# An attention and mixture-of-experts kernel: wk moved to the front of SyncE's queue, q before v in the first batch, and the differences of the rounded chunks moved from GpSimd to VectorE

## The reference, cut to what matters

```python
x = x + xattn(layernorm(x), ctx_768, Wq, Wk, Wv, Wo, bo)   # 8 batches of 256 tokens, width 256, context width 192, 4 heads
x = x + ffn(layernorm(x), ...)

def xattn(q, kv, ...):
    qp, kp, vp = q @ Wq.T, kv @ Wk.T, kv @ Wv.T            # split in 4 heads of 64
    attn = softmax(einsum('bhqd,bhkd->bhqk', qh, kh) * 64 ** -0.5)
    return merged(attn @ vh) @ Wo.T + bo

def ffn(x, ...):                                           # 2048 tokens, 32 experts, 4 chosen for a token
    scores = softmax(xf @ gw + gb)                         # 8 groups of 4 experts; the best 4 groups are kept,
    weights, indices = top4 of the kept experts            # then the best 4 experts
    y = sum over chosen experts of weight * ((silu(xf @ w1 + b1) * (xf @ w3 + b3)) @ w2 + b2)
    z = (silu(xf @ sw1 + sb1) * (xf @ sw3 + sb3)) @ sw2 + sb2     # the shared expert, for every token
    return y + z
```

## Time and profile before

| what | value |
|---|---|
| median of 3 executions | 361.5 us (359.2 to 362.98) |
| the profiled execution, its time | 360.53 us |
| the profiled execution, its span | 358.8 us |
| busy share of PE, DVE, ACT, POOL | 88%, 71%, 54%, 50% |
| mean granted TensorE clock | 0.957 of full speed |
| DMA | 68.96 MB, 192 GB/s in the mean |

### The profile page before, as it was taken

The page is one execution under the profiler, slowest core; times in us unless marked ns, Lnnn a source line. Parts: engine busy times, 40 slices in busy tenths (PEclk is TensorE's granted clock), DMA queues, the critical chain, the costliest instruction groups (busy, mean ns, idle before and its releaser), DMA issues.

```text
span 358.8 us, 9631 instructions
## 1 busy us (share of the span) xinstructions
PE 314.1 (88%) x2240; PEld 265.0 (74%) x2241; DVE 255.0 (71%) x865; ACT 194.1 (54%) x632; POOL 179.8 (50%) x221
## 2 busy tenths in 40 slices
PE   2998999999999999799999999999999999996000
PEld 1785887978788787478877888998989898985000
DVE  5489777878787785964795666776676676764775
ACT  2386777878777576327312565665656565653000
POOL 4620402656555575715562065666666576656500
PEclk9999999999999999699999999999999999999655
DMA  6899265585822236402424355656666565658798
GB/s 175 264 395 377 82 202 178 221 287 185 311 74 91 76 127 241 172 18 76 143 93 124 99 171 170 194 175 195 184 192 185 167 212 171 191 179 306 272 412 301
DMA packets 33782, 68.96 MB, mean 192 GB/s; under 512 B 5339, under 2 KB 26108, under 8 KB 32092
## 3 DMA queue, kind: packets, MB, share of 16 engines
q1 hardware_dynamic: 26364, 46.95, 40.6%
q0 software_dynamic: 6960, 21.11, 15.9%
q10 hardware_dynamic: 432, 0.59, 0.6%
HBM read 39.87 MB, written 28.77 MB: 191 GB/s over the span
## 4 chain that ended last, share of the span: by engine, by line
PE 76%; DMA 9%; DVE 5%; issue 3%; ACT 2%; SPq 2%; ACTq 1%; POOL 0%; POOLq 0%; DVEq 0%
PE psS L1235 11%; PE psF L103 7%; PE psF L1244 5%; PE psS L1224 5%; PE psF L1235 5%; DMA xn2T_all<-dispatch 4%; PE psS L103 4%; PE psS L985 4%; PE psF L1020 4%; PE psS L993 4%; PE psF L1034 3%; PE psF L939 3%; PE psF L1127 3%; PE psS L1093 3%; DMA w<-shares 2%
## 5 line engine op out<-in xcount | busy, mean ns | idle before, releaser
L677 POOL DMA_INDIRECT shares<-xn2T_all,e_number x81 | 86.2, 1064 | 60.1 <-issue 25.5
L626 POOL DMA_INDIRECT dispatch<-work,slot_now x64 | 64.7, 1010 | 59.2 <-issue 22.2
L1235 PE MATMUL psS<-work,arena 128*128 128x128 f32 x432 | 57.1, 275 | 0.0
L1235 PEld LDWEIGHTS psS<-work,arena 128*128 128x128 f32 x432 | 52.6, 192 | 0.1
L904 ACT ACTIVATE work<-psS 128x256 f32<-128x256 f32 x81 | 30.9, 383 | 17.8 <-PE psS L1224 14.7
L1670 DVE SCALAR_TENSOR_TENSOR work<-psS,b,work 128x128 f32<-128x128 f32 x54 | 18.9, 351 | 27.6 <-ACT work L915 27.3
L1673 DVE COPY arena<-w 128x512 f32 x81 | 35.1, 434 | 2.5 <-issue 2.5
L1224 PE MATMUL psS<-ident,xn2T_all 128*128 128x128 f32 x162 | 31.6, 278 | 3.3 <-DMA xn2T_all<-dispatch 2.2
L1244 PE MATMUL psF<-w,work 128*128 x108 | 32.5, 382 | 0.5 <-DVE work L1670 0.5
L915 ACT ACTIVATE work<-psS,b 128x128 f32<-128x128 f32 x54 | 19.8, 367 | 24.1 <-PE psS L1235 23.1
L1224 PEld LDWEIGHTS psS<-ident,xn2T_all 128*128 128x128 f32 x162 | 21.3, 141 | 15.0 <-DMA xn2T_all<-dispatch 3.9
(11 more groups left out here) (233 smaller groups left out, 778.4 us busy)
## 6 DMA issues: line engine op xcount, KB each, us to landing
xn2T_all<-dispatch SPq DMA_DIRECT2D x81, 160.0 KB, 2.3
w<-in_w SPq DMA_DIRECT2D x6, 1536.0 KB
w<-shares SPq DMA_DIRECT2D x6, 1024.0 KB, 7.7
dispatch<-padding SPq DMA_DIRECT2D x8, 640.0 KB, 9.7
w<-in_w SPq DMA_DIRECT2D x1, 2304.0 KB
w<-shares SPq DMA_DIRECT2D x3, 512.0 KB, 7.0
out<-x SPq DMA_DIRECT2D x3, 512.0 KB, 3.4
hs_ctx<-in_ctxT SPq DMA_DIRECT2D x7, 192.0 KB, 3.2
```

The source lines that it names most:

```text
L626: pool.indirect_dma_start(dispatch, bass.IndirectOffsetOnAxis(ap=slot_now[:, par, n:n + 1], axis=0), xn2[:, par, n // TOPK, :], None).then ...
L677: pool.indirect_dma_start(shares, bass.IndirectOffsetOnAxis(ap=e_number[:, u:u + 1], axis=0), e_y[:, u, :], None).then_inc(added[u], 16)
L1235: ins = pe.matmul(hidden_bank(u)[:, m * P:(m + 1) * P], e_w13k[:, u % UNROLL, k, m * INTER:(m + 1) * INTER], e_xT[:, u % 3, k, :], start=( ...
```

## The change

In the head, the load of wk moves from the second place of ACT's queue to the first place of SP's, in front of x0; PE does q before v, and ACT copies q out before v.

In the shared expert's stage, ACT does `weights_out(0)` and `weights_now(1)` inside the last attention step, in front of `silu(1, 1)` and the roundings of chunks 3 to 5, and no longer behind them. The five `split_chunk` leave GpSimd for VectorE: chunk 3 and, in front of it, `shared_hidden(1)` stand right behind the choice of the experts of batch 6, chunk 4 where `shared_hidden(1)` stood, chunk 5 behind `norm2(7)`, chunk 6 behind the weights of batch 7, and chunk 7 behind the ranks of batch 7.

In the diff, the first block is SyncE's; then come GpSimd's (the old `split_chunk` and its calls), ScalarE's (from `else:` to `q_out`, `v_out` and the loop over chunks), TensorE's (`norm_T(0)` to `proj_v(0, 0)`) and VectorE's (the new `split_chunk` and its calls in `norm2` and behind it).

```diff
+            sp.dma_start(wk[0:KC], a["wk"]).then_inc(s["wk_in"], 16)
             sp.dma_start(x[:, 0:TPB, :], xv[:, 0:TPB, :]).then_inc(s["x0_in"], 16)
...
-            def split_chunk(c):
-                pool.wait_ge(s["chunk_rounded"], c - WHOLE + 1)
-                rest(xn2_low[c % 3][:, :, :], xn2T_all[:, c], xn2_high[c % 3][:, :, :], "chunk_split")
...
-            split_chunk(3)
-            split_chunk(4)
-            split_chunk(5)
...
-            split_chunk(6)
-            split_chunk(7)
...
                 else:
+                    weights_out(0)
+                    weights_now(1)
                     silu(1, 1)
                     for c in range(WHOLE, 6):
                         round_chunk(c)
...
-            act.dma_start(wk[0:KC], a["wk"]).then_inc(s["wk_in"], 16)
             act.dma_start(wv[0:KC], a["wv"]).then_inc(s["wv_in"], 16)
...
             norm_out(0)
+            q_out(0)
             v_out(0, 0)
-            q_out(0)
...
-                if c != 2:
+                if c not in (0, 2):
                     weights_out(c)
-                if c + 1 < BATCHES:
+                if 1 <= c and c + 1 < BATCHES:
                     weights_now(c + 1)
...
             norm_T(0)
+            pe.wait_ge(s["wq_in"], 16)
+            proj_q(0)
             pe.wait_ge(s["wv_in"], 16)
             proj_v(0, 0)
-            pe.wait_ge(s["wq_in"], 16)
-            proj_q(0)
...
+            def split_chunk(c):
+                dve.wait_ge(s["chunk_rounded"], c - WHOLE + 1)
+                dve.tensor_tensor(xn2_low[c % 3][:, :, :], xn2T_all[:, c], xn2_high[c % 3][:, :, :].bitcast(F32), ALU.subtract).then_inc(s["chunk_split"], 1)
...
                     route_chosen()
+                if not attended:
+                    shared_hidden(1)
+                    split_chunk(3)
...
                 if not attended:
-                    shared_hidden(1)
+                    split_chunk(4)
...
             norm2(last, 1, True, attended=False)
+            split_chunk(5)
             shared_add(0)
...
             route_weights(last, 1)
+            split_chunk(6)
             shared_add(2)
...
+            split_chunk(7)
             shared_add(3)
```

## The result

The changed kernel takes 356.75 us in the median of 20 executions (354.85 to 358.44), the kernel before 359.56 (20 executions, 356.31 to 363.2). The ratio is 0.9931, 95% interval 0.9903 to 0.9958. All ratios here leave out executions more than 1.5% above the fastest of the same kernel as disturbed; where many of one kernel's executions are left out so, the ratio can differ from that of the medians by up to 0.6%. The profiled execution takes 355.4 us with a span of 353.6, against 360.53 and 358.8: 5.1 us less, nearly twice the difference of the medians.

What follows compares the result with a forecast made beforehand. TensorE's own sequence, 76% of the chain of waits, was taken as the bound. 360.53 - 5.85 (hole and clock) + 0.3 (head) = 355.0, plus 1.0 for the median, gave 355.9 us; range 353.0 to 359.8.

Steps and rivals of the forecast that it cites:

- The start: Base of the sum: profiled 360.53 us, plus 1.0 because the median of the executions before lay that far above it.
- The hole: TensorE idle from 144.31 to 146.72, waiting for ScalarE's copy cwT; the earlier copy was to remove it, gaining 2.41 us.
- The clock behind it: TensorE's clock near half level right after the idle time; was to stay full, gaining 3.4 us (bounds 0 to 3.4).
- Rival (b): Clock's fall absent from all or some executions of before's median; only the idle time counts: 359.4 us, chance 0.15.
- VectorE keeps ahead: With the differences moved to it, VectorE has batch 7's normalised rows ready before TensorE's norm2_T(7), slack 1.1 us.
- The two stalls: VectorE's 4.08 us instruction beside GpSimd's differences and 2.42 us rounding; about 3.9 and 2.0 us of them were to go.
- Cost nothing: The differences' move to VectorE was to add no time on TensorE's path, given slack of 1.1 us.
- The head: wk ahead of x0 and q before v: norm_T(1) and what follows later by 0.3 us, between -1.7 and +3.
- rival (a): Idle times in the head keep TensorE's clock low until 17.4 or later: 358.1 us, chance 0.17.
- The weighed rule: Head loads: transfers from different engines interleave, so wk lands 0.8 us sooner, x0 0.5 later, and the head comes out even.
- The clock's starting level: TensorE starts throttled despite the clock column's 1.00; before, it stayed at the lower level until about 14.1.
- The gain carries to the end: Expert loop's loads and TensorE's first transposes there both move along, so the 5.85 us persists to the end.

Runs made afterwards that it cites:

- tail edit: Kernel before with only the shared expert's stage changed (ScalarE's two copies earlier, five differences on VectorE), old head: ratio 0.9875, repeated on another chip 0.9876.
- experiment 1: The changed kernel with its head undone, against the kernel before: ratio 0.9875; repeated 0.9876, 2.0 us faster than the changed kernel on the same chip.
- experiment 4: Kernel before plus five unused multiplications in shared_down(0), filling TensorE's idle time in front of its products: ratio 0.9960 to before.
- experiment 5: Kernel before with one part of the stage's edit each: ScalarE's two copies moved alone, ratio 0.9981; five differences on VectorE alone, 0.9949.
- experiment 3: Three heads on the tail edit, ratios to the kernel before: wk first with v before q 0.9907; old loads with q before v 0.9871; wk behind x0 0.9834.

## Why the prediction was right or wrong

The measured 356.75 lies 0.85 us above the forecast and inside the range; the sign was right, the size was not: 5.6 us forecast against before's first median of 361.5, and 2.8 measured between the medians of 20. That the time came out near is luck. The start of the sum was 1.9 us too high, while the head's loss was taken 1.7 us too small and the tail edit's gain about 1.0 us too large, and these nearly cancel. (The last two go by the head's 2.0 us of experiment 1: 359.56 - 356.75 + 2.0 = 4.8 us for the tail edit, an estimate.)

- **The start.** 1.0 us was added because the median of the first three executions lay above the profiled one. With 20 executions before's median is 359.56, 1.0 below it.
- **The hole, 2.41 us.** Right: gone in the profile, and in the third group's profile of the tail edit alone.
- **The clock behind it, 3.4 us.** The mechanism is shown (experiment 4), and so is the size in a profiled execution (5.7 us for hole and clock). In the medians it depends on the occasion: by experiment 4 the clock is worth some 1.5 us on the first chip, where the low level lasted 3.4 us and not 6.8, and the whole tail edit 6.2 us in the third group, where nothing is missing from 5.85. Rival (b), given 0.15, had the fall in none or only some of the median's executions; no run shows how many have it.
- **VectorE keeps ahead.** Right: slack 1.5 us. The two stalls were gone as forecast (0.17 us where it was 4.08, 0.43 where it was 2.42). "Cost nothing" understated the edit's role, though: without it the hole only moves (experiment 5). The step to see beforehand was that `shared_hidden(1)`, behind VectorE's stalls, becomes what TensorE waits for.
- **The head, +0.3 us.** The term that failed most. 1.4 us in the profile, 2.0 in the median. x0 landed at 5.8, where 5.3 was worked out and 5.9 was the bound, which puts the transposes at 10.6 in place of 10.2. The low clock lasted until about 15.7 in one profile and past 18 in the other (estimates from the durations of q and v), where 14.1 was taken, and 1.6 us more at half speed are 0.8 us. The 14.1 was the moment of one profile, and even the old head's lies some 3 us earlier in another execution (experiment 3). All this points the way of rival (a), which had 1.7 to 2.7 us more than the forecast.
- **The weighed rule** of the Trainium skill, "DMA: Bandwidth & Descriptors", section "Issuing engines are not separate DMA queues", would have had wk at 6.1 and x0 at 4.1. The traces differ: on SyncE's queue wk is there by 4.86 and x0 not before 5.8. The place within one queue decides here, more than the rule says.
- **The clock's starting level** in the Trainium skill's "TensorE: Matmul & The Clock Gate", section "What's actually happening": by that rule, the trace agrees again, since line 956 takes 3.75 us for eight products at a clock column of 1.00.
- **The gain carries to the end.** Right: 4.3 us at the loop's start, 5.2 in the span.

## What to carry to other kernels

An idle time in front of a dense stretch of TensorE can cost more than its length, but do not price the clock's part from one profile: here the low level behind the same hole lasted 3.4 us in one profile and 6.8 in another. Several profiles, and the spread of many executions, say how much of it the median has. When a wait is removed, follow the next awaited engine through its own queue: here either half of the edit alone left a hole somewhere, and both together removed it. In a head that is bound by loads, ask for each transfer that is moved forward which one then lies behind it, and don't pull a consumer (q) ahead of the work that hid its wait (v). Don't judge a change of some tenths of a microsecond there by one profile: the same head moved by 1.9 us from execution to execution.

## What the runs showed of the hardware

- Behind 2.06 to 2.46 us without work TensorE's granted clock fell to the 1.2 GHz level in all seven cases of the profiles; with the 2.41 us of before filled by products whose result nobody uses it stayed up. It stayed up behind 1.54 or 1.55 us, too, in all twelve cases in front of batch 2's transposes. Once 1.78 us, and once 1.31 us soon after another short wait, were enough for a fall. The low level then lasted 3.4 us in six of these nine cases and 6.8 us in three. On the first chip the clock fell three more times, later in the kernel, behind several short waits.
- From the first product to full speed TensorE took between about 4 and 7 us in seven profiles with the same head, without idle time in between (an estimate from the durations).
- VectorE's instruction on 128x2 elements took 4.08 us while three of GpSimd's 128x512 subtractions ran back to back, and 0.17 without them. In the profile of ScalarE's move alone the same instruction began in the midst of three such subtractions and took 1.10 us, so it can get in between.
- 192 KB in front of x0's 256 KB on one queue put x0's first use from 3.6 to 5.8 us (5.4 to 6.0 in four profiles); behind x0, the same 192 KB let the first product begin at 5.97 against 7.04 with the old head on that chip and left x0 at 3.7.
- The same kernel took 359.56, 360.4 and 360.7 us in the median on three occasions and 384.3 us on another chip, where ScalarE took up the copy of `cwT` 1.45 and 2.2 us late in two profiles. The tail edit's ratio was 0.9875 there and 0.9876 on another chip, but its median lay 3.5 us below before's there and 6.2 on the other, so the ratios agree better than the kernels do.
